# Seventh layer: the two normalisation steps of a round take other places in its order

## The reference, cut to what matters

```python
x = x + jnp.tanh(g_ffn[2]) * _L2_ffn_ref(_layernorm(x, axis=-1), ...)      # sixth: experts, top 1
x = x + jnp.tanh(g_xattn[3]) * _L3_xattn_ref(_layernorm(x, axis=-1), ctx_1024, ctx_1024, ...)

def _L3_xattn_ref(query, key, value, Wq, Wk, Wv, Wo):      # 16 heads of 64
    q, k, v = heads(query @ Wq), heads(key @ Wk), heads(value @ Wv)
    scores = q @ k.T / sqrt(64)
    return merge(softmax(scores) @ v) @ Wo
```

## Time and profile before

| | us |
|---|---|
| three runs | 3958.63 (median), 3945.28, 3960.69 |
| the profiled execution's own time | 3959.01 |
| its span in the trace | 3956.3 |
| mean granted TensorE clock | 0.866 of full speed |

### The profile page before, as it was taken

How to read it: one execution, slowest core, us unless ns; L and a number is a source line. 1 busy time by engine, 2 the same in 40 slices (tenths; PEclk the granted TensorE clock), 3 DMA queues, 4 the chain that set the end, 5 groups by cost and what they waited for, 6 DMA issues and landing times.

```text
span 3956.3 us, 106820 instructions
## 1 busy us (share of the span) xinstructions
PE 3214.9 (81%) x39458; PEld 2495.8 (63%) x39458; DVE 2607.1 (66%) x7302; ACT 1752.1 (44%) x4103; POOL 1160.3 (29%) x1193
## 2 busy tenths in 40 slices
PE   6999978888886999976689957766287999999955
PEld 5888854555553666656689945555286777777744
DVE  5677746777775787874454458888423666666679
ACT  4766744555553444432233312222043665665611
POOL 2222223333332333326520024443801223222211
PEclk9999988999997777867799977786599999999966
DMA  3000010000001000011147731110163000000000
GB/s 96 8 9 8 8 24 8 7 7 7 7 7 72 18 17 17 18 15 38 36 168 254 252 111 34 35 32 9 52 217 109 14 11 12 12 11 13 7 17 25
DMA packets 165933, 180.23 MB, mean 46 GB/s; under 512 B 45824, under 2 KB 142848, under 8 KB 165120
## 3 DMA queue, kind: packets, MB, share of 16 engines
q1 hardware_dynamic: 139728, 139.20, 10.8%
q0 software_dynamic: 25600, 28.64, 2.6%
q10 hardware_dynamic: 432, 10.19, 0.6%
HBM read 65.58 MB, written 33.03 MB: 25 GB/s over the span
## 4 chain that ended last, share of the span: by engine, by line
PE 37%; issue 24%; DVE 18%; POOL 9%; DMA 5%; ACT 2%; SPq 2%; another core or an unknown queue 2%; DVEq 0%; POOLq 0%; ACTq 0%
PE ps L965 31%; PE ps L1179 4%; DMA scr_y<-acc 3%; POOL probs L943 3%; DVE mx L1934 2%; POOL arena_a L931 2%; POOL route L937 1%; POOL rstd L920 1%; POOL scr L906 1%; DVE probs L1936 1%; PE ps L1016 1%; DVE den L1947 1%; DVE xn L1844 1%; DVE mx L1923 1%
## 5 line engine op out<-in xcount | busy, mean ns | idle before, releaser
L943 POOL TENSOR_TENSOR probs<-probs,den 128x1024 f32<-128x1024 f32 x128 | 243.2, 1901 | 768.6 <-DVE den L1949 768.6
L965 PE MATMUL ps<-small,xcT 128*64 128x64 f32 (+6 forms) x2976 | 409.6, 355 | 56.1 <-DVE oT L2042 19.7
L1590 ACT ACTIVATE pT<-ps 128x512 f32<-128x512 f32 (+1 forms) x576 | 305.0, 572 | 206.7 <-PE ps L1179 203.9
L965 PE MATMUL ps<-small,oT 128*64 128x128 f32 (+1 forms) x2304 | 326.0, 292 | 28.4 <-ACT oT L1598 16.9
L1179 PE MATMUL ps<-small,probs 128*128 128x128 f32 x2176 | 323.9, 293 | 8.2 <-ACT pT L1590 4.7
L965 PEld LDWEIGHTS ps<-small,oT 128*64 128x64 f32 (+1 forms) x2304 | 279.8, 152 | 75.1 <-ACT oT L1598 24.4
L1598 ACT ACTIVATE oT<-ps 64x512 f32<-64x512 f32 x512 | 288.9, 588 | 78.5 <-PE ps L965 75.5
L1179 PEld LDWEIGHTS ps<-small,probs 128*128 128x128 f32 x2176 | 257.1, 149 | 101.6 <-issue 40.5
L920 POOL TENSOR_TENSOR rstd<-veps,neghalf 128x2 f32<-128x2 f32 (+1 forms) x192 | 147.6, 769 | 576.8 <-DVE veps L1836 382.6
L965 PE MATMUL ps<-arena_b,qT 64*64 64x64 f32 (+3 forms) x10056 | 282.7, 232 | 29.9 <-DVE probs L1920 24.6
L931 POOL DMA_DIRECT2D arena_a<-kT x416 | 216.7, 527 | 279.8 <-ACT kT L1531 263.1
(11 more groups left out here) (291 smaller groups left out, 7454.8 us busy)
## 6 DMA issues: line engine op xcount, KB each, us to landing
wbuf<-parts SPq DMA_DIRECT2D x70, 704.0 KB, 3.5
wbuf<-parts_b SPq DMA_DIRECT2D x39, 512.0 KB, 3.0
scr_y<-acc SPq DMA_DIRECT2D x109, 128.0 KB, 3.4
xcT<-in_ctxT SPq DMA_DIRECT2D x96, 128.0 KB
arena_a<-kT SPq DMA_DIRECT2D x608, 8.0 KB
xcT<-scr SPq DMA_DIRECT2D x70, 128.0 KB, 2.2
arena_a<-kT POOLq DMA_DIRECT2D x416, 8.0 KB
xn<-scr SPq DMA_DIRECT2D x39, 128.0 KB, 2.2
```

The source lines that it names most:

```text
L943: pool.tensor_tensor(pr, pr, rv[:, t, 0:nh].unsqueeze(2).to_broadcast([P, nh, S]), ALU.mult).then_inc(s_probs.sem, 1)
L965: return nc.tensor.matmul(o, lhsT, rhs, start=start, stop=stop, skip_group_check=True)
L1590: nc.scalar.activation(pT[:, t, 4 * j:4 * j + n, :].rearrange("p c t -> p (c t)"), bank(b, n * P), ACT.Copy).then_inc(drained[b], 1)
```

## The change

In `make_layers`, the order of the seventh layer's items: `L++` moves from the 21st place to the first, and `M++` from the 24th place to between `K0+` and `N1`. All other items keep their order. No instruction is added or removed.

```diff
     l3x = Layer(6, "l3x", stages(
-        "F+ T0- S0 T1- P0 S1 Q2+ N0 Q0+ A0- K2+ Q1+ V0+ A1- P1 K0+ N1 W0- Q3+ K3+ L++ V2+ W1- M++ V3+ K1+ V1+"),
+        "L++ F+ T0- S0 T1- P0 S1 Q2+ N0 Q0+ A0- K2+ Q1+ V0+ A1- P1 K0+ M++ N1 W0- Q3+ K3+ V2+ W1- V3+ K1+ V1+"),
         attention, (6, 7), 16, 64 ** -0.5, True)
```

## The result

The changed kernel takes 3972.74 us (median of 19 runs, 3964.19 to 3984.94), the kernel before 3960.12 us (19 runs on the same chip, 3939.15 to 3974.51). The ratio is 1.0034, with a 95% interval of 1.0021 to 1.0047: slower by 8 to 19 us. Forecast were 3944 us and a gain, with a range of 3927 to 3959.

A forecast was written before the change was run, and what follows sets the result against it. TensorE was taken as the bound, busy 21.21 of 22.60 us a round. 29 x 0.57 = 16.5 us less, plus 1.6 for the first rounds, gave -14.9 from 3959.01: 3944 us, range 3927 to 3959.

The forecast's parts named there:

- GpSimd's queue: Root and two gathers move from the round's end to +2.0 up to about +5.3; 3.5 us stay free, no cost.
- rival 3: Statistics stand in full between F and the softmax, adds held again: slower, 3982 us; chance 0.07.
- The wait before F: At the round's end, F held by V1 alone, starting 0.57 us earlier in each steady round.
- L at the head: Statistics at the round's start take 2.03 us instead of 3.10; the maximum could start at +2.50, scores come at +2.57.
- The step that I trusted least: At the round's head, the vector queue is free just in time for S0's maximum, with 0.07 us to spare.
- The root beside `c_parts`: At the round's head, GpSimd's root does not lengthen `c_parts`: zero taken; if held, 0.33 us per round.
- M: Its 0.60 us goes into 1.66 us of vector engine idle time before N1's sum, costing nothing there.
- The first rounds: In rounds -1 and 0, the first `xlo` waits for a gather, 4.6 us late; net +1.6 us.
- The sum: 29 steady rounds save 0.57 us each, 16.5 in all; with +1.6 from the first rounds, -14.9 us.

The follow-up runs named there:

- e3: Changed kernel with only the first of a group's two gathers, the second tile's expert rows left out: 3943.51 us, one run.
- e5: Changed kernel with the gathers behind GpSimd's multiplication for N1 and one group further ahead than in e1: 3934.49 us, ratio to the kernel before 0.9943.
- e7: Changed kernel with the two indirect gathers replaced by direct copies of 64 KB each from the same queue: 3936.91 us, one run.
- e8: Changed kernel with M back at its old place behind W1, L still at the head: 3980.89 us, one run.
- e1: Changed kernel with the two gathers moved behind GpSimd's multiplication for N1, fetching the same group later in the round: ratio to the kernel before 1.0036.
- e2: Changed kernel with GpSimd waiting for S0's maximum before it issues the gathers: 3965.48 us, one run.
- e10: Kernel before with the two transfers triggered by S0's scores and made as direct copies: 3884.57 us, one run; the kernel before took 3888 on that occasion.
- e6: As e3, with the one gather held until S0's scores are complete: 3939.2 us, one run.
- e9: Changed kernel with the first gather left at the head and the second behind GpSimd's multiplication for N0: ratio to the kernel before 0.997.

## Why the prediction was wrong

**GpSimd's queue: the step that failed.** The prediction moved the root and two gathers to +2.0 up to +5.3, counted the room on GpSimd ("3.5 us are free"), and costed the move at nothing. The room was there, and nobody waited for GpSimd. It asked only who waits for the moved instructions and what is queued behind them, not what runs beside them at the new place: the 64 small matmuls of S1. The price is 1.27 us in each of 27 rounds, 34.3 us. The trace of the kernel before held not only the neighbour but the price, in two rounds that the prediction did not look at. In most rounds the second gather lies beside F and T0. But the round from 3048.15 has no T0, and there it lies beside S0:

```profile
3048.49 1.00 POOL L839 DMA_INDIRECT ctx_sb<-scr_y,meta  x1 [0.30 <-issue]
3048.52 0.92 PE L965 MATMUL ps<-arena_b,qT 64*64 64x64 f32 x46
...
3049.81 1.48 PE L965 MATMUL ps<-arena_b,qT 64*64 64x64 f32 x82 [0.37 <-issue]
...
3051.22 0.39 PE L965 MATMUL ps<-xhi,q_parts 128*128 128x256 f32 x1
```

This is the one pause of 0.4 us that the waits of the kernel before list. The 128 matmuls take 2.70 us to Q2; in the changed kernel, which has no gather beside them in that round, they take 2.02. So one gather cost 0.68 us there. In the round from 3541.77 a gather came 0.45 us late, ran into S0, and S0 took 1.38 us in place of 1.16. As an estimate from the first of these, two gathers beside S1 cost 2 x 0.68 = 1.36 us, less the 0.3 that V0's wait takes up, near 1.1 a round: the sign and most of the size. A bound for it was missing from the range, and none of the rivals had this mechanism; rival 3 had the sign, and by luck nearly the time (3982 against 3972.74), for a reason that didn't happen.

**The wait before F: right.** F follows V1 at once (3187.53 to 3188.54), no wait is left, and undisturbed rounds are 21.92 us (e3, e5, e7); the forecast was 22.00.

**L at the head: right, nearly to the clock.** Times from F, forecast and measured: `veps` +1.73 and +1.72, `xlo` +1.8 and +1.80, `c_parts` +2.15 and +2.15, the maximum +2.50 and +2.49. The adds take 0.60. The step that I trusted least held.

**The root beside `c_parts`: right.** The root runs from 3190.51 to 3191.22 and `c_parts` lies wholly in it, from 3190.69, with 0.42 us, against 0.41 before. (The subtraction of the earlier trace rows only starts inside its root: it ends at 2408.22, 0.13 behind it. The prediction has it as running inside.) The Trainium skill, page "SBUF — State Buffer", section "Who interferes with whom", would have held it; the trace disagrees for this pair too.

**M: right.** The idle time before N1's sum shrank from 1.66 to 1.15 us and nothing was late; e8, with M at its old place, has the same round within 0.06 us.

```profile
3204.65 1.22 DVE L1947 TENSOR_REDUCE den<-probs 128x16 f32<-128x1024 f32 x1 [1.15 <-ACT probs L1584]
```

**The first rounds: right in kind.** The first `xlo` waits for the gather, as forecast:

```profile
3036.29 0.66 PE L1016 MATMUL ps<-small,xn 128*128 128x128 f32 x2 [11.41 <-DVE xn L1844]
...
3039.98 0.61 DVE L1794 SCALAR_TENSOR_TENSOR x_sb<-ctx_sb,meta,x_sb 128x128 f32<-128x128 f32 x2 [3.59 <-DMA ctx_sb<-scr_y,meta]
...
3042.09 0.42 DVE L1971 TENSOR_TENSOR xlo<-ps,xhi 128x256 fp32r<-128x256 f32 x1
```

It starts 5.80 us after F; before, the first F was at 3032.39, and `xlo` 1.18 after it: 4.6 later, as forecast. The two rounds from that F on take 36.26 us (3036.29 to 3072.55) in place of 35.26: +1.0, where +1.6 was forecast.

**The sum.** The 29 rounds after that take 670.15 us (3072.55 to 3742.70) against 654.63, +15.5, and with the first two +16.5; the medians differ by 12.6, within an interval of 8 to 19. From the forecast of -14.9 this trace is a miss of 31.4 (the measured median is 28.7 above the forecast): 34.3 for the pauses, less 2.3 because undisturbed rounds are 21.92 and not 22.00 (29 x 0.08), less 0.6 for the first rounds. Of the other 4.6 us between the two spans, 3.9 lie ahead of the layer's first F, and 3.85 of them already ahead of its first gather; the change has no part in those.

## What to carry to other kernels

A moved step has three lists, not two: what is behind it on its queue, who waits for it, and **what runs beside it** at the new place, on every engine. An instruction that nobody waits for can still cost time by its company. In this kernel indirect gathers belong beside the long matmuls and not beside a run of 64 tiny ones, and the moment to choose is free if their data is fetched a round ahead: that turned a loss of 0.3% into a gain of 0.6%. An odd single row in the list of waits, here one pause of 0.4 us that no semaphore ended, is worth a look before anything is moved. And where an undo puts an instruction later, first count when its data is wanted, as e1 shows.

## What the runs showed of the hardware

TensorE can be stopped by what GpSimd does, with no semaphore between them. Beside the issue of indirect gathers (1.0 to 1.1 us each), a run of 64x64 matmuls, which starts one each 17 ns undisturbed (64 in 1.09 us), stands still up to three times, with 5 or 6 matmuls between two pauses. The profile labels 0.24 to 0.5 us of each as "issue"; from start to start they are 0.45 to 0.7 us. The weight loads pause with the matmuls, for 0.5 us. It happened in S1, in A0 (e2), and in S0 in the kernel before. Beside matmuls of 128x256 and 128x512 no pause was seen (e2's first gather, e5), and beside direct copies from the same queue neither (e7, e10, and the earlier layer of the kernel before, where 128 matmuls start one each 14 ns).

The Trainium skill says in the section "Who interferes with whom" of "SBUF — State Buffer" that "PE and ACT never wait on anyone". That sentence is about the ports of SBUF, and no run here shows that the pauses come from a port. Taken more widely, as a reader might, the trace disagrees, by 21.3 us in 54 pauses.

Why is open. That the weight loads stop too, and that the dense runs suffer and the long matmuls don't, would fit a shortage in the supply of instructions to TensorE, and GpSimd's work for an indirect gather could be what delays that supply. This is argued, not shown: no run changed how TensorE gets its instructions. The trace rules out one form of it, that new instructions are loaded by DMA in each round. From 3118 to 3720 us, 26 rounds with 50 pauses, the changed kernel's trace has only eight packets of instructions (its list of DMA queues: `q14 instruction: 8, 0.07, 0.0%`).

The runs don't say either how the pauses depend on the number of rows in a gather, why a gather that ends 0.6 us into S1 (e3) costs it 0.24 to 0.28 us and one 0.35 later (e6) 0.57, nor why the same gather costs nothing in e9.
